# First attention of a two-layer kernel: softmax sums over four column tiles of 32, and the products beside it over every second step

## What is computed

```python
q = quat_norm(quat_linear(x, qW, qb))        # 16 heads of 64
k = quat_norm(quat_linear(x, kW, kb))
v = quat_linear(x, vW, vb)
scores = einsum('bhtd,bshd->bhts', q, k) * scale + mean(sin(J)) * 0.1
attn = softmax(scores)                       # over all 4096 keys
x = layernorm(x + quat_linear(einsum('bhts,bshd->bthd', attn, v), oW, ob))
# FFN: x and the weight are rounded to a 6-bit grid in blocks of 32
x = layernorm(x + quantize(x) @ quantize(weight).T + bias)
```

## Time and profile before

| | us |
|---|---|
| median of three runs | 2383.06 (2376.89 to 2389.04) |
| profiled execution | 2379.78 |
| its slowest core, span | 2378.2 |
| its other cores | 2365.1 to 2377.4 |
| keys, queries, values | 0 to 309.3 |
| tiles 0, 1, 2, 3 | 262.5, 298.3, 297.2, 299.5 |
| tile 4 | 107.3 |
| the rest | 804.1 |

### The profile page before, as it was taken

One profiled execution on the slowest core, in us unless ns is written; L12 is line 12 of the kernel. 1 busy time (PEld: TensorE's weight loads), 2 busy tenths in 40 slices (PEclk: granted clock), 3 DMA queues, 4 the chain that ended last, 5 costly groups with the idle time before them and its releaser, 6 DMA issues.

```text
span 2378.2 us, 42634 instructions; the slowest of 8 cores (2365.1 to 2378.2 us)
## 1 busy us (share of the span) xinstructions
PE 2029.0 (85%) x14618; PEld 820.9 (35%) x14618; DVE 1077.7 (45%) x1569; ACT 1594.7 (67%) x2143; POOL 407.6 (17%) x254
## 2 busy tenths in 40 slices
PE   5999999999999999999999998787477777877765
PEld 2444432222222222222222223443244444444443
DVE  6565567412354313643136432553245555555541
ACT  1434279999888898989989898642156555555542
POOL 3000000010000200002000010100014553554553
PEclk9999999999999999999999999898779898899997
DMA  6423220210100101001010010461440101101100
GB/s 98 81 53 58 36 74 23 79 36 5 41 15 20 65 6 41 14 21 65 6 37 12 19 63 2 83 104 49 108 90 28 36 19 37 37 19 37 37 19 27
DMA packets 63854, 101.00 MB, mean 42 GB/s; under 512 B 25617, under 2 KB 46225, under 8 KB 62242
## 3 DMA queue, kind: packets, MB, share of 16 engines
q1 hardware_dynamic: 41138, 67.77, 9.1%
q0 software_dynamic: 22512, 30.51, 7.9%
HBM read 88.86 MB, written 22.02 MB: 47 GB/s over the span
## 4 chain that ended last, share of the span: by engine, by line
PE 44%; ACT 20%; DVE 12%; issue 10%; POOL 8%; DMA 3%; SPq 2%; ACTq 0%; DVEq 0%; POOLq 0%
ACT TE L686 16%; PE PALL L1065 12%; PE PALL L1114 6%; PE PALL L1092 6%; PE PALL L1078 6%; PE PALL L1096 4%; PE PALL L1250 3%; POOL TX L615 3%; PE PALL L1187 2%; PE PALL L1153 2%; ACT TY L701 2%; POOL TY L618 2%; DVE TY L950 2%; SPq L485 1%; POOL TY L627 1%
## 5 line engine op out<-in xcount | busy, mean ns | idle before, releaser
L686 ACT ACTIVATE TE<-PALL,BIASB 128x1024 bf16<-128x1024 f32 x1088 | 1124.3, 1151 | 125.8 <-PE PALL L1078 123.0
L1078 PE MATMUL PALL<-TE,TY 64*128 64x512 bf16 (+1 forms) x2560 | 430.0, 352 | 89.7 <-ACT TE L686 52.0
L1092 PE MATMUL PALL<-TE,TY 128*64 128x512 bf16 (+1 forms) x2560 | 457.8, 372 | 3.7 <-DVE TY L948 3.7
L1096 PE MATMUL PALL<-TE,TY 128*64 128x512 bf16 (+1 forms) x2560 | 434.2, 353 | 0.0
L1078 PEld LDWEIGHTS PALL<-TE,TY 64*128 64x128 bf16 x2560 | 134.8, 93 | 551.8 <-issue 549.1
L701 ACT ACTIVATE TY<-PALL,SMALL 128x384 bf16<-128x384 f32 x272 | 155.4, 579 | 120.8 <-DVE SMALL L975 113.9
L1092 PEld LDWEIGHTS PALL<-TE,TY 128*64 128x64 bf16 x2560 | 143.7, 110 | 235.6 <-issue 225.7
L564 POOL TENSOR_TENSOR TX<-TX 128x1024 f32<-128x1024 f32 x17 | 39.9, 2348 | 951.6 <-DVE TY L877 951.6
L1114 PE MATMUL PALL<-TE,TY 128*128 128x512 bf16 x544 | 168.8, 401 | 36.3 <-DVE TY L913 23.5
L947 DVE COPY TY<-PALL 128x512 f32<-128x512 f32 (+1 forms) x40 | 24.4, 610 | 367.8 <-PE PALL L1096 367.8
L1187 PE MATMUL PALL<-TY 128*128 128x512 bf16 x544 | 149.2, 431 | 38.1 <-POOL TY L624 36.8
(11 more groups left out here) (127 smaller groups left out, 2319.3 us busy)
## 6 DMA issues: line engine op xcount, KB each, us to landing
TE<-WOD SPq DMA_DIRECT2D x5, 2048.0 KB, 8.5
TE<-FWD SPq DMA_DIRECT2D x5, 2048.0 KB, 7.9
TX<-XST SPq DMA_DIRECT2D x17, 512.0 KB, 3.7
TY<-Y2SP POOLq DMA_DIRECT2D x17, 512.0 KB, 3.5
YOUT<-TY SPq DMA_DIRECT2D x17, 512.0 KB, 2.6
Y2SP<-TY SPq DMA_DIRECT2D x17, 256.0 KB, 2.2
TE<-XF POOLq DMA_DIRECT2D x8, 512.0 KB, 10.6
TY<-XF POOLq DMA_DIRECT2D x8, 512.0 KB, 10.2
```

The costliest lines, as they stand in the source:

```text
L686: s.activation(EXPS(m), PB(2 * (m % 2), 0, 1024), AF.Exp, bias=BIASB[:, 63:64], scale=0.125).then_inc(*up("exp", m))
L1078: op = t.matmul(PB(2 * (m % 2) + hh, x * w, w), KB(c, (s * k + x) * 128, 128, 64 * hh, 64), QB(c, 0, w, 64 * hh, 64), start=True, stop=Tru ...
L1092: t.matmul(PB(6, 0, w)[64 * hh:64 * hh + 64, :], VB(s * k + x, (2 * c + hh) * 64, 64), EXPS(m)[:, hh * 512 + x * w:hh * 512 + x * w + w], ...
L1096: op = t.matmul(PB(7, 0, w)[64 * hh:64 * hh + 64, :], ONEB, EXPS(m)[:, hh * 512 + x * w:hh * 512 + x * w + w], start=first, stop=last, til ...
```

## The change

It has three parts.

First, the sums. ONEB has 32 columns. The exponentials of a step, 1024 columns, are taken as four groups of 256, and four matmuls, each in 32 columns of the array, sum them into rows 32g to 32g+31 of bank 7. Groups 0 and 1 hold the first head's queries, 2 and 3 the second's. For tile 4 a step's four key blocks of two heads are summed as 256 columns each too, and the two halves are added later.

Second, att_out. The denominators now lie in another layout than the numerators. VectorE copies 256 columns of sums, takes the reciprocal of 256, and copies the result with eight copies of 32 rows x 256 columns into the layout of the numerator, then multiplies. In tile 4 it adds two halves, moves them by four copies of 32 x 128, adds again, takes the reciprocal and multiplies. TensorE's V products of a new head pair wait for the copy of the numerator (pvn), its sums for the copy of the sums (pvf).

Third, the plan. chunk() has a distance d: the eight parts of a product stand at every d-th step. In a tile of 512 queries d is 2, with o = 8+16j and b = 88+32j; in tile 4 and behind d is 1, at the old offsets.

```diff
-    def chunk(T, j, o, b, e1, e2):
+    def chunk(T, j, o, b, d):
+
         put("pool", o, "xb", T, j)
         for i in range(8):
-            put("pe", o + i, "o", T, j, i)
-        put("dve", o + 9, "z1", T, j)
-        put("act", o + min(14, e1 - 1), "r1", T, j)
-        put("dve", o + e1, "n1", T, j)
+            put("pe", o + d * i, "o", T, j, i)
+        z = o + 7 * d + 2
+        put("dve", z, "z1", T, j)
+        put("act", z + 2 + 2 * d, "r1", T, j)
+        put("dve", z + 3 + 3 * d, "n1", T, j)
         put("dve", b, "quant", T, j)
         put("pool", b + 8, "xf", T, j)
         put("pe", b + 10, "t", T, j)
         put("dve", b + 11, "tev", T, j)
         for i in range(8):
-            put("pe", b + 13 + i, "f", T, j, i)
-        put("dve", b + 22, "z2", T, j)
-        put("act", b + min(27, e2 - 1), "r2", T, j)
-        put("dve", b + e2, "n2", T, j)
-        put("sp", b + e2, "y2", T, j)
+            put("pe", b + 13 + d * i, "f", T, j, i)
+        z = b + 13 + 7 * d + 2
+        put("dve", z, "z2", T, j)
+        put("act", z + 3 + d, "r2", T, j)
+        put("dve", z + 2 + 3 * d, "n2", T, j)
+        put("sp", z + 2 + 3 * d, "y2", T, j)
...
-            for j, o in enumerate((10, 20, 36, 46)):
-                chunk(T - 1, j, B + o, B + 72 + 32 * j, 18, 33)
-            put("sp", B + 56, "wld", T - 1, "f")
-            put("sp", B + 192, "wld", T, "o")
             for j in range(4):
-                put("sp", B + 106 + 32 * j, "xld", T, j)
+                chunk(T - 1, j, B + 8 + 16 * j, B + 88 + 32 * j, 2)
+            put("sp", B + 73, "wld", T - 1, "f")
+            put("sp", B + 220, "wld", T, "o")
+            for j in range(4):
+                put("sp", B + 128 + 32 * j, "xld", T, j)
...
-        ONEB = bview(TY2, 65536, 64)
+        ONEB = bview(TY2, 65536, 32)
...
                 v.tensor_copy(NM, PB(6, 0, w)).then_inc(*up("pvn", T, c))
-                v.tensor_copy(DN, PB(7, 0, w)).then_inc(*up("pvf", T, c))
+                SUM = TQ[:, 0:256]
+                v.tensor_copy(SUM, PB(7, 0, 256)).then_inc(*up("pvf", T, c))
                 v.wait_ge(*at("pvf", T, c))
-                chain(v.reciprocal(DN, DN))
...
-                v.tensor_tensor(ATT(T, c)[:, 0:w], NM, DN, ALU.mult).then_inc(*up("att", T, c))
+                if w == 512:
+                    REC = ATT(T, c).bitcast(F32)
+                    chain(v.reciprocal(REC, SUM))
+                    for q in range(4):
+                        for half in (0, 1):
+                            src = 32 * (q // 2 * 2 + half)
+                            op = v.tensor_copy(TQ[32 * q:32 * q + 32, 256 * half:256 * half + 256], REC[src:src + 32, :])
+                    chain(op)
+                    v.tensor_tensor(ATT(T, c), NM, TQ, ALU.mult).then_inc(*up("att", T, c))
+                else:
+                    OWN, OTHER = TQ[:, 0:128], TQ[:, 128:256]
+                    chain(v.tensor_tensor(OWN, OWN, OTHER, ALU.add))
+                    for q in range(4):
+                        src = 32 * (q ^ 1)
+                        op = v.tensor_copy(OTHER[32 * q:32 * q + 32, :], OWN[src:src + 32, :])
+                    chain(op)
+                    chain(v.tensor_tensor(OWN, OWN, OTHER, ALU.add))
+                    chain(v.reciprocal(OWN, OWN))
+                    v.tensor_tensor(ATT(T, c)[:, 0:w], NM, OWN, ALU.mult).then_inc(*up("att", T, c))
...
                 if s == 0 and m:
-                    t.wait_ge(*at("pvf", T if c else T - 1, (c - 1) % 8))
+                    t.wait_ge(*at("pvn", T if c else T - 1, (c - 1) % 8))
...
-                    for hh in (0, 1):
-                        op = t.matmul(PB(7, 0, w)[64 * hh:64 * hh + 64, :], ONEB,
-                                      EXPS(m)[:, hh * 512 + x * w:hh * 512 + x * w + w],
-                                      start=first, stop=last, tile_position=(0, 64 * hh))
...
+                if s == 0 and m:
+                    t.wait_ge(*at("pvf", T if c else T - 1, (c - 1) % 8))
+                for g in range(4):
+                    op = t.matmul(PB(7, 0, 256)[32 * g:32 * g + 32, :], ONEB, EXPS(m)[:, 256 * g:256 * g + 256],
+                                  start=(s == 0), stop=(s == SPP[T] - 1), tile_position=(0, 32 * g))
```

14 lines of the change are left out of this document (7 added, 7 removed).

## The result

The changed kernel takes 2440.4 to 2447.8 us, the kernel before 2376.9 to 2389.0: a ratio of 1.0252, 95% interval 1.0221 to 1.0284. The profiled execution took 2445.1 us, its slowest core has a span of 2443.2.

What follows compares the result with a forecast made beforehand. ScalarE's exponentials in the first attention were taken as the bound, delayed by TensorE's product steps and a loop through VectorE. Terms -21+20+3+6 = +8 on the median 2383.1 gave 2391 us, range 2354 to 2413.

Steps and rivals of the forecast that it cites:

- the sum: Whole kernel: -21+20+3+6 = +8 us on the median of 2383.1, giving 2391 us.
- second stretches: Steps 80 to 207 of tiles 1 to 3, beside the FFN products: 30.1 us lost per tile, against 23.4; +20 us.
- the head ends of tile 0 and of the last steps: Eight head ends in tile 0 and one each in tiles 1 to 3, each 0.3 us longer: +3 us.
- tile 4: Last tile: att_out 3.6 us instead of about 2.0 in three waits, +4.8, head ends +1.2; +6 us, bounds 0 and 9.
- The price of the change of shape: TensorE, V to sums: 0.10 us for the new change of array shape, bounds 0 and 0.10; plain step 0.86.
- first stretches: Steps 0 to 79 of tiles 1 to 3, beside the output projection: 9.9 us lost per tile, not 17.0; -21 us.
- Rival B: TensorE's change from 64 to 32 columns is free: step 0.76, pair 2.05, sum -35, 2348 us; chance 0.17.
- The two large terms: Tiles 1 to 3: -21 us in steps 0 to 79 and +20 us in steps 80 to 207.
- The sums' term: Sums' cost outside the steps: head ends elsewhere 0.3 us each, +3, and tile 4's longer att_out and head ends, +6.
- the loop of the second stretch: VectorE chain between FFN chunks, steps 80 to 207: chain 23.3 us, loop 39.0 against 32.1, plus 1.4 for the clock.
- Rival C: The eight att_out copies on VectorE cost 0.34 us each: +15, clock +5, 2411 us; chance 0.20.
- the things to watch: New-profile signs: spacings 0.32 and 0.22, first 80 steps about 90 us, next 128 about 158, nine tev waits about 3.

Runs made afterwards that it cites:

- the kernel with the scores twice: Changed kernel with the score matmuls of the steps that have scores alone written twice, same result: 2432.6 us twice.
- the order has slack: Quantizing 20 steps earlier, transposes and copy before the head's end, products on both sides: 2320.0 to 2325.0 us with old sums, 2356.7 to 2367.3 with the change's.
- the two controls: Scores of scores-only steps written twice in the kernel before (2374.0, 2377.7 us) and in that kernel with the change's sums (2406.1, 2407.3, 2436.6 us).

## Why the prediction was wrong, point by point

**Where the 54 us are.** By the table's rows the change costs 62 us where the sum had 8. Of the 54 between, 24 are in the second stretches (+44, forecast +20), 13 in the first (-8, forecast -21), 9 at the head ends of tile 0 and of the last steps (+12, forecast +3) and 8 in tile 4 (+14, forecast +6).

**The price of the change of shape was right.** I took 0.10 us for V to sums, with a plain step of 0.86 and three caught-up steps of 1.62. Measured: 0.09 to 0.10 over the old spacing, 0.88, and 1.68 (514.47 to 516.15 in the kernel with the scores twice, whose sums are the change's). The 0.02 between 0.86 and 0.88 are 4 of the 13 us in the first stretches (64 steps, three tiles; an estimate). The rule that the Trainium skill gives on its page TensorEngine Tiling (Array Packing), section Tiling Modes, is that a change of mode, and not just of the tile, drains the engine. The traces agree: V to sums is 0.33 us where the modes differ and 0.22 where they don't. Rival B's figures for a free switch (0.76 a step, 2.05 a pair of steps) are what the kernel with V in tiles of 32 shows (0.76, 2.06).

**The two large terms hold for the order, and not for what was changed.** -21 and +20 were worked out for the order and the sums together; together they are -8 and +44. With the old sums the order shows -15.8 and +19.8. What they say of the order is right within some 5 us; the sums are missing from them.

**The sums' term was the wrong one.** Beside their price in the steps I gave them +3 for head ends and +6 for tile 4. They cost 51 us of span beside the same order; the rows of the table, each a median of its own, add up to 57. Of these 20 are in the second stretches and go when the order has slack (24.2 against 4.2); 13.5 are tile 4; the rest, some 23, is in tile 0 (6.0), the first stretches (7.6), the last steps (5.6) and what is left of the second. Of that rest 32 head ends at 0.27 and 96 pairs of steps at 0.02 to 0.03 more would be some 11 us, an estimate from the spacings, and some 7 the lower clock, the difference of the two controls. These parts come from different kernels; some 5 us stay without an account.

**The step that failed first was the loop of the second stretch.** I sized the chain at 23.3 us and the loop at 39.0, with 1.4 for the clock 40.4; on the slowest core the nine loops take 41.2 to 44.8, 42.5 on average. The 2.1 us too little in each of nine loops are 19 of the 24. att_out was 6.20 us instead of 5.4, since the copies took 0.30 us each and not the 0.21 that I took from a row of another shape (0.8 a loop); one loop of each tile had 3.79 to 5.93 us for the eight instead of 2.38, where GpSimd's adds ran beside them, which I had written off ("over before the copies begin", which is true of xf, while it is the xb of the next tile's chunks that stands there; 0.9 a loop on average); tev to the product was 1.32 instead of 0.94 (0.4). The waits were 4 to 8 us instead of 3, the lower clock came after each, and a loop's first pair of steps took 3.2 to 3.5 us instead of 2.25; the 1.4 for the clock covers that. Each is small and each counts in full, because nothing in that loop has room. With no copies at all the stretches take 43 us less.

**Rival C** had the right mechanism and condition: it was to decide from 0.25 us a copy, and they took 0.30 (0.35 on average over the kernel). Its 15 us were the price of the 0.13 us a copy that C put above the forecast's 0.21, plus 5 for the clock. Set against the 43 that all copies are worth, the whole price by C would be 96 copies at the twelve hand-overs, 33 us at 0.34 each, and 20 us at 0.21. They were 37 us long, with GpSimd's adds beside three of the twelve sets, and worth 43. So C had the copies within a quarter, and the second stretches nearly right (by its terms 20+13+5 = +38, measured +44). For the other 30 of the 54 us, in the first stretches, at the head ends and in tile 4, it had 2 us more than the forecast.

**Tile 4** was sized as three VectorE chains of 1.6 us and 1.2 for head ends, upper bound 9. It costs 13.5 to 14.4 with V in tiles of 64, 9 to 11 with V in 32: VectorE's end of a head, 3.95 us instead of 2.0, comes eight times in 64 steps, and it counts at more than three of them: against the order alone, the exponential behind a head's end comes more than 1 us later at six (7.6 us instead of 4.2 at one). Some 4 us of the row are the copies of tile 3's last head's end, which I had not counted there (118.9, without the copies 114.9). What the other parts do was not tried.

**The clock at head ends** was not in the sum at all outside the second stretch. In the kernel before it held at nearly all head ends of tile 0, and I took that for given; after the change it falls at three in ten.

**The range** ended at 2413, 2 us above C's own value. It took in the bounds of single costs but not that three of them meet in one loop. Of the things to watch, the spacings came (V to sums 0.33 and sums to scores 0.23, forecast 0.32 and 0.22), copies over 0.25 us apart, which was C's sign, and a lower granted clock in the second stretches (0.93 to 0.95, before 0.98 to 0.99). The first 80 steps of a tile took 95 us and not about 90, the next 128 took 167 and not about 158, and the waits for tev in tiles 1 to 3 were twelve of 4.5 us on average, not nine of about 3.
